# Ten embedding sums on one core: x loaded in pieces of up to eight tiles, through a ring of 24 tiles, with three converted buffers

## The reference

```
embs    = [x @ w for x, w in zip(xs, ws)]
emb_sum = sum(embs)
q_emb   = sum((x ** 2) @ (w ** 2) for x, w in zip(xs, ws))
fm_ans  = 0.5 * (emb_sum ** 2 - q_emb)
return concatenate([fm_ans] + embs, axis=-1)
```

## Time and profile before

| | |
|---|---|
| Median of 3 runs | 285.73 us |
| Profiled execution | 285.67 us, span 283.9 us |
| Bytes moved | 113.88 MB, mean 401 GB/s |
| Busy: DVE, ACT, PE, POOL | 240.3, 227.6, 218.4, 88.1 us |
| Chain that ended last | DMA 63%, "issue" 23%, DVE 6%, ACT 3% |
| Mean granted TensorE clock | 0.987 |

### The profile page before, as it was taken

How to read it: one execution, slowest core, us unless ns; L and a number is a source line. 1 busy time by engine, 2 the same in 40 slices (tenths; PEclk the granted TensorE clock), 3 DMA queues, 4 the chain that set the end, 5 groups by cost and what they waited for, 6 DMA issues and landing times.

```text
span 283.9 us, 2928 instructions
## 1 busy us (share of the span) xinstructions
PE 218.4 (77%) x878; PEld 154.2 (54%) x878; DVE 240.3 (85%) x236; ACT 227.6 (80%) x271; POOL 88.1 (31%) x68
## 2 busy tenths in 40 slices
PE   0459989998887878888687778778778778777791
PEld 0338657776565655555465555555555555545561
DVE  3752999999999989988789988988988988888874
ACT  0769999999978878878887877877877878778762
POOL 0432427317234124107244044044044044004000
PEclk9998999999999999999999999999999999999997
DMA  7999999999999999999999999999999999999972
GB/s 234 396 404 415 407 417 415 420 413 418 416 422 418 419 423 413 419 417 420 413 421 415 420 421 417 421 423 414 418 422 419 416 418 415 418 413 420 410 304 99
DMA packets 22417, 113.88 MB, mean 401 GB/s; under 512 B 3728, under 2 KB 4752, under 8 KB 10752
## 3 DMA queue, kind: packets, MB, share of 16 engines
q1 hardware_dynamic: 16976, 106.90, 91.5%
q10 hardware_dynamic: 5424, 6.79, 6.7%
HBM read 110.79 MB, written 2.88 MB: 400 GB/s over the span
## 4 chain that ended last, share of the span: by engine, by line
DMA 63%; issue 23%; DVE 6%; ACT 3%; PE 2%; POOL 1%; ACTq 1%; DVEq 0%; POOLq 0%
DMA x_ring<-in_x_dram 58%; DVE is_one L450 5%; DMA whole<-in_w_dram 5%; ACT is_set L296 2%; PE sums L385 1%; ACT turned L307 1%; POOL low L366 1%; PE sums L392 1%; DVE total L487 0%; ACT whole L289 0%; ACTq L276 0%; POOL high L364 0%; DVE results L490 0%; DVE results L493 0%; ACTq L283 0%
## 5 line engine op out<-in xcount | busy, mean ns | idle before, releaser
L450 DVE TENSOR_SCALAR_CACHE_REDUCE is_one<-x_ring 128x2048 uint8<-128x2048 f32 (+2 forms) x108 | 226.2, 2114 | 29.0 <-DMA x_ring<-in_x_dram 28.8
L296 ACT ACTIVATE is_set<-x_ring 128x2048 fp32r<-128x2048 uint32 (+2 forms) x108 | 192.2, 1784 | 37.2 <-DMA x_ring<-in_x_dram 37.1
L385 PE MATMUL sums<-is_set,low 128*128 128x512 f32 x398 | 134.8, 420 | 59.6 <-ACT is_set L296 52.7
L385 PE MATMUL sums<-is_set,high 128*128 128x512 f32 x398 | 125.9, 398 | 0.0
L385 PEld LDWEIGHTS sums<-is_set,low 128*128 128x128 f32 x398 | 68.4, 191 | 104.2 <-ACT is_set L296 54.3
L385 PEld LDWEIGHTS sums<-is_set,high 128*128 128x128 f32 x398 | 75.9, 191 | 17.5
L364 POOL CAST high<-whole 128x1024 fp32r<-128x1024 f32 (+5 forms) x31 | 27.0, 871 | 170.5 <-ACT whole L289 170.5
L366 POOL TENSOR_TENSOR low<-whole,high 128x1024 fp32r<-128x1024 f32 (+5 forms) x31 | 60.6, 1953 | 2.5
L296 ACT ACTIVATION_READ_ACCUMULATOR is_set<-x_ring 128x1 f32 (+1 forms) x108 | 20.7, 192 | 0.0
L289 ACT ACTIVATE whole<-whole 128x512 f32<-128x512 f32 (+5 forms) x31 | 16.8, 541 | 4.1 <-DMA whole<-in_w_dram 4.1
L392 PE MATMUL sums<-identity,turned 128*128 128x128 f32 x80 | 11.2, 286 | 0.8 <-ACT turned L337 0.8
(11 more groups left out here) (17 smaller groups left out, 3.7 us busy)
## 6 DMA issues: line engine op xcount, KB each, us to landing
x_ring<-in_x_dram SPq DMA_DIRECT2D x91, 1024.0 KB, 18.3
x_ring<-in_x_dram SPq DMA_DIRECT2D x16, 512.0 KB, 10.2
whole<-in_w_dram ACTq DMA_DIRECT2D x19, 256.0 KB, 7.5
out_dram<-results SPq DMA_DIRECT2D x10, 256.0 KB, 12.4
x_ring<-in_x_dram SPq DMA_DIRECT2D x1, 448.0 KB, 6.5
whole<-in_w_dram ACTq DMA_DIRECT2D x2, 192.0 KB, 5.7
whole<-in_w_dram ACTq DMA_DIRECT2D x2, 160.0 KB, 7.2
out_dram<-results ACTq DMA_DIRECT2D x1, 256.0 KB, 2.1
```

Of the source, the lines that this page charges most:

```text
L296: nc.scalar.activation(is_set[chunk.k % SETS][0:chunk.rows, 0:chunk.n * BATCH], x_of(chunk).bitcast(U32), ACT.Sign, accum_out=set_counts[0 ...
L385: last = nc.tensor.matmul(sums[:, summing(n, half), :], w, x[0:chunk.rows, at:at + HALF], start=first, stop=False, skip_group_check=True)
L450: nc.vector.tensor_scalar(is_one[chunk.k % 2][0:chunk.rows, 0:chunk.n * BATCH], x_of(chunk), 1.0, None, ALU.is_equal, ALU.add, accum_out=o ...
```

## The change

Three things change. First, a load of x holds all chunks of a group, up to eight tiles, in rows of up to 32 KB; the tail of a table, and every chunk of the last table, stay loads of their own. There are 42 loads in place of 108, numbered 0 to 41. Chunks are as before, and so is what DVE, ACT, POOL and PE do with them and in what order. Second, the ring is 24 tiles long, and loads of any length stand in it one behind another; where the next one doesn't fit to the end, it begins again at tile 0. A load waits until every earlier load that shares a tile with it is counted whole (`free`). A load has one of 12 semaphores, and DVE and ACT wait for the whole load before its first chunk. Third, `is_set` has 3 buffers: ACT may write chunk k once chunk k - 3 is multiplied.

```
-SLOTS = 8
-SETS = 5
+LOAD = 8
+RING = 24
+LANDS = 12
+SETS = 3
...
+def plan_loads():
+    lists = []
+    for group in GROUPS:
+        joined = []
+        for chunk in group.chunks:
+            if joined and (chunk.tail or group.table == LAST or sum(c.n for c in joined) + chunk.n > LOAD):
+                lists.append(joined)
+                joined = []
+            joined.append(chunk)
+        lists.append(joined)
+    loads, at = [], 0
+    for i, chunks in enumerate(lists):
+        at = 0 if at + sum(chunk.n for chunk in chunks) > RING else at
+        loads.append(Load(i, chunks, at))
+        at += loads[-1].n
+        loads[-1].free = max([o.end for o in loads[:-1] if o.at < at and loads[-1].at < o.at + o.n] +
+                             [o.end for o in loads[:-1] if o.land == loads[-1].land] + [0])
+    return loads
...
-            for chunk in CHUNKS:
-                if chunk.k >= SLOTS:
-                    sp.wait_ge(ones_counted, chunk.k - SLOTS + 1)
-                    sp.wait_ge(set_counted, chunk.k - SLOTS + 1)
-                at = chunk.tile * BATCH
-                sp.dma_start(x_of(chunk),
-                             x_end[chunk.table] if chunk.tail else
-                             x_dram[chunk.table][:, at:at + chunk.n * BATCH]
-                             ).then_inc(x_landed[chunk.slot], 16)
+            free = 0
+            for load in LOADS:
+                if load.free > free:
+                    free = load.free
+                    sp.wait_ge(ones_counted, free)
+                    sp.wait_ge(set_counted, free)
+                at = load.tile * BATCH
+                sp.dma_start(in_ring(load.at, load.n)[0:load.rows],
+                             x_end[load.table] if load.tail else
+                             x_dram[load.table][:, at:at + load.n * BATCH]
+                             ).then_inc(x_landed[load.land], 16)
...
             def count_set(chunk):
-                act.wait_ge(x_landed[chunk.slot], 16 * (chunk.turn + 1))
+                act.wait_ge(x_landed[chunk.load.land], 16 * (chunk.load.turn + 1))
```

More of the change, by code:

```diff
@@ L60, in __init__ @@
         self.k, self.table, self.tile, self.n, self.at = k, table, tile, n, at
-        self.slot, self.turn = k % SLOTS, k // SLOTS
         self.tail = tile + n == TILES[table]
         self.rows = TAIL[table] if TILES[table] == 1 else P
-        self.group = None
+        self.group = self.load = None
+class Load:
+    def __init__(self, i, chunks, at):
+        self.chunks, self.at, self.i = chunks, at, i
+        self.table, self.tile, self.tail = chunks[0].table, chunks[0].tile, chunks[0].tail
+        self.n, self.rows = sum(chunk.n for chunk in chunks), chunks[0].rows
+        self.end = chunks[-1].k + 1
+        self.land, self.turn = i % LANDS, i // LANDS
+        for chunk in chunks:
+            chunk.load, chunk.within = self, chunk.tile - self.tile
 class Group:
@@ L100 @@
 NGROUPS, NCHUNKS = len(GROUPS), len(CHUNKS)
+def plan_loads():
[16 more added lines that the diff above has]
+    return loads
+LOADS = plan_loads()
 G_ORDER = [9] + [t for t in range(NT) if t != 9]
@@ L132, in rec_kernel @@
         sums = ctx.enter_context(nc.psum_tensor("sums", [P, NB, 512], F32))
-        x_ring = sb("x_ring", [P, SLOTS * CHUNK * BATCH], F32)
+        x_ring = sb("x_ring", [P, RING * BATCH], F32)
         is_set = [sb(f"is_set{i}", [P, CHUNK * BATCH], F32R) for i in range(SETS)]
@@ L160, in rec_kernel @@
         w_landed = [sem(f"w_landed{i}") for i in range(WHOLES)]
-        x_landed = [sem(f"x_landed{s}") for s in range(SLOTS)]
+        x_landed = [sem(f"x_landed{s}") for s in range(LANDS)]
         x_multiplied = sem("x_multiplied")
@@ L193, in rec_kernel, with in_ring @@
         block = ctx.enter_context(nc.Block())
-        def in_slot(slot, elements):
-            at = slot * CHUNK * BATCH
-            return x_ring[:, at:at + elements]
+        def in_ring(tile, n):
+            return x_ring[:, tile * BATCH:(tile + n) * BATCH]
         def x_of(chunk):
-            return in_slot(chunk.slot, chunk.n * BATCH)[0:chunk.rows]
+            return in_ring(chunk.load.at + chunk.within, chunk.n)[0:chunk.rows]
         def part_of(group, part):
@@ L246, in _ @@
                             sp.wait_ge(g_multiplied, base + i + 1)
-                            sp.dma_start(in_slot(0, BATCH), x_dram[t][:, bass.ds(i * BATCH, BATCH)]
+                            sp.dma_start(in_ring(0, 1), x_dram[t][:, bass.ds(i * BATCH, BATCH)]
                                          ).then_inc(gx_landed, 16)
@@ L251, in _ @@
                     sp.wait_ge(g_multiplied, base + end + 1)
-                    sp.dma_start(in_slot(0, BATCH)[0:x_end[t].shape[0]], x_end[t]).then_inc(gx_landed, 16)
+                    sp.dma_start(in_ring(0, 1)[0:x_end[t].shape[0]], x_end[t]).then_inc(gx_landed, 16)
                     w_end, before = w_dram[t][:, end * D:TILES[t] * D], P - rows if end else 0
@@ L427, in _ @@
                         block_b = slice(b * P, (b + 1) * P)
-                        nc.tensor.matmul(sums[:, b, 0:D], in_slot(0, BATCH)[:, block_b],
+                        nc.tensor.matmul(sums[:, b, 0:D], in_ring(0, 1)[:, block_b],
                                          g_weights[:, 0, :], start=True, stop=True,
                                          skip_group_check=True)
-                        last = nc.tensor.matmul(sums[:, b, D:2 * D], in_slot(1, BATCH)[:, block_b],
+                        last = nc.tensor.matmul(sums[:, b, D:2 * D], in_ring(1, 1)[:, block_b],
                                                 g_weights[:, 1, :], start=False, stop=True,
@@ L445, in count_ones @@
             def count_ones(chunk):
-                dve.wait_ge(x_landed[chunk.slot], 16 * (chunk.turn + 1))
+                dve.wait_ge(x_landed[chunk.load.land], 16 * (chunk.load.turn + 1))
                 if chunk.k >= 2:
@@ L507, in _ @@
                 dve.wait_ge(x_multiplied, NCHUNKS)
-                g_link(nc.vector.memset(in_slot(0, BATCH), 0.0))
+                g_link(nc.vector.memset(in_ring(0, 1), 0.0))
                 nc.vector.nop().then_inc(g_multiplied, 1)
@@ L519, in add_tile @@
                         dve.wait_ge(gw_landed, 16 * (base + i + 1))
-                        x, w = in_slot(0, BATCH), g_weights[:, 0, :]
-                        nc.vector.tensor_tensor(in_slot(1, BATCH), x, x, ALU.mult
+                        x, w = in_ring(0, 1), g_weights[:, 0, :]
+                        nc.vector.tensor_tensor(in_ring(1, 1), x, x, ALU.mult
                                                 ).then_inc(gx_ready, 1)
```

## The result

The changed kernel takes 299.12 us (median of 4 runs, 298.7 to 300.88) against 285.84 us before beside it: a ratio of 1.0473, interval 1.0425 to 1.0521. The forecast was 296 (286.5 to 302). The profiled execution has a span of 298.9 us, 15.0 more than before; it took 300.88 us, 1.8 more than the median of its kernel, so what is read from its trace adds up to some 15 and not to 13.3.

The account below looks back on a forecast made before the run. It took moving 113.7 MB by DMA as the bound. Its terms, -5.5 + 3.9 + 4.5 + 3.0 + 4.7 = +10.6 us on 285.67, gave 296.3, stated as 296, range 286.5 to 302.

Parts of the forecast that it names:

- the mechanism it took as likeliest: Whole kernel: weights wait by turns behind 32 KB rows of x, so ACT waits; 296 us, chance 0.55.
- the change of tables: From table 1 to table 0: ACT waits 7.6 us for weights, load 25 starts late, engines idle 3.9 us.
- Fewer packets: DMA queues: 42 x loads instead of 108 save 9,504 packets, 5.5 us less DMA time.
- the fit of two equations: Two hardware queues' packets, MB and busy shares solved for cost: 9.3 ns per packet, 37.4 us per MB on an engine.
- Weights behind longer rows: Weight loads of 256 KB beside x: landing goes from 7.5 to about 15 us, bounds 7.5 and 23.
- Who waits: ACT, squaring weights in order: no lasting wait in long tables, but losses at table 1's end, the start and group 29.
- the start: Early groups: ACT or DVE delays hold back load 17 and idle the DMA, 0 to 9 us, 4.5 taken.
- Group 29: Weights in three parts take 19 us against 14.2; ACT waits 5, reaches the last eight 3 us late: 3.0 us.
- Tail: End of kernel: chunks 97 to 100 land together, ACT needs 18.0 us to chunk 107, 4.7 us more than before.
- Three is_set: ACT waiting for PE to free one of three buffers: 0 to 3 us if PE's clock halves, 0 taken.

Follow-up runs that it names:

- eights only in the middle: Changed kernel with loads of eight only in groups 10 to 26, chunk by chunk elsewhere, weights of groups 12 to 30 in x's queue: 285.14 us.

## Why the prediction was right

It was right in direction, in size (13.3 us measured, 10.3 forecast) and in the mechanism it took as likeliest, with two terms of its sum off by some 2 us each, both to the fast side, and one (the change of tables) whose size came out by luck. By its steps:

- *Fewer packets*, -5.5 us: the count was right, the gain too large, 3.3 us of packet time (256.5 against 259.8). What failed is the fit of two equations, carried on to rows four times as long: it took 9.3 ns off each packet saved, where loads of four, 6,336 packets fewer, saved 259.8 - 255.3 = 4.5 us, 11 ns each, and the 3,168 that eights save on top saved nothing. Rows above 16 KB bring nothing more here; why is open.
- *Weights behind longer rows*, 15 us: 14.0 measured, 9.9 for 16 KB rows (9.7 by the same sum), 7.4 for 8 KB rows in a load of eight tiles. It is the row that counts, and one for one. The rule of whole packets of 9 to 17 descriptors (the Trainium skill, DMA: Bandwidth & Descriptors, section Queues, rings and completion order) was read in the forecast as 9 to 14 us for the eights, so the 14.0 does not decide. Nor do the 9.9 and 7.4: a transfer of x puts eight rows on each engine in all these kernels, so a wait for one whole transfer and nine turns behind single rows come to nearly the same. What decides is the 32 packets of each queue between 185 and 187.5 us: turns of single rows, against that rule.
- *Who waits.* ACT lost 22.8 us ("20 or more"), the start 5.2 us of holes (4.5 taken, 0 to 9 the bounds) and shorter loads or shorter rows took them away. The change of tables was forecast at 3.9 us. The pauses found there are 2.6 us by packets (1.6 by windows); the 3.5 by difference hold everything behind the start. So the size was about met, but by luck: ACT waited 2.99 us there and not 7.6, because its sequencer issued the weights at 134.36, a chunk ahead of where I had it, and the pause stays where no weights are late (three of the experiments: rows of 8 KB, weights in x's queue, eights only in the middle). What is left is the eights', and most likely that of the ring shifted by one tile.

```profile
134.36 0.35 ACTq L318 DMA_DIRECT2D whole<-in_w_dram  x1
...
146.48 0.63 ACT L331 ACTIVATE whole<-whole 128x512 f32<-128x512 f32 x1 [2.99 <-DMA whole<-in_w_dram]
```

- *Group 29*, 3.0 us: ACT came 2.9 us late, after a wait of 5.04 (5 forecast).
- *Tail*, 4.7 us: 18.1 us from landing to last chunk without late weights, 18.0 forecast.
- *Three is_set*, taken at 0 with a bound of 3: this was mis-sized, by 2 us. The bound named the case (PE at half clock after a wait for weights), and it came true from 268 us on, where ACT then waited 1.8 us for PE.

Together: -3.3 + 5.2 + 3.5 + 2.9 + 4.7 + 2.1 = +15.1, against 15.0 in the profiled span and 13.3 between the medians. The 3.5 is what is left when the others are taken off, so the sum closes by construction up to the landing; from there on each term is read, the 2.1 as what ACT took from 267.97 to 288.12, 20.1 us, above the forecast 18.0. Why runs of the changed kernel differ by 2.2 us stays open.

## What to carry to other kernels

Before loads are joined, price two things that a DMA share of 1.0 does not show. Everything that waits for a load, or is freed by it, comes in one piece: the last load is worked off after it lands, and a ring can run dry until the room for one whole piece is free (8 of the 13 us here, tail and ring together). And a longer row lets every small transfer beside it wait longer, turn by turn: list those transfers, their rows per engine and the time between issue and use, and stop at the row length that still fits (16 KB here, 1% faster, where 32 KB was 5% slower).

## What the runs showed of the hardware

- Two queues shared the DMA engines by rows, one of each by turns, though one queue's were 32 KB and the other's 2 KB: 32 packets of each moved between 185 and 187.5 us. So 256 KB of weights landed in 7.4, 9.9 and 14.0 us beside rows of 8, 16 and 32 KB.
- In the steady part rows of 16 KB reach 424 GB/s and rows of 32 KB 424, where rows of 8 KB reach 418 to 419.
- After PE had stood idle for 5.15 us in the changed kernel it ran at its lower granted clock, 1.2 GHz (two matmuls took 1.05 us in place of 0.62); the mean over the span was 0.913 against 0.987. Met with three buffers in the tail this cost some 2 us, 1.8 of them in waits of ACT for PE.
